# Another order of the last rows of a layered graph kernel, with later steps for the chunk that is third from the end

## What is computed

```python
x = _layernorm(x + relu((adj @ x) @ kernel + bias))
u, v = x, None
for _ in range(3):
    v = mlp_uv(adj @ u)      # three layers 128 -> 128, each with bias and leaky relu
    u = mlp_vu(adj @ v)
return _layernorm(x + v)     # over the 128 features of a node
```

## The kernel before

| row | steps | closes at | hid1 | hid2 | out | statistics |
|---|---|---|---|---|---|---|
| 4 | LAST | 1500 | 1506 | 1510 | 1514 | 1516 |
| 3 | LATE2 | 1516 | 1520 | 1523 | 1525 | 1528 |
| 1 | LATE | 1524 | 1527 | 1529 | 1531 | 1538 |
| 2 a | END | half of the last block | 1535 | 1539 | 1543 | 1549 |

## Time and profile before

### The profile page before, as it was taken

How to read it: one execution, slowest core, us unless ns; L and a number is a source line. 1 busy time by engine, 2 the same in 40 slices (tenths; PEclk the granted TensorE clock), 3 DMA queues, 4 the chain that set the end, 5 groups by cost and what they waited for, 6 DMA issues and landing times.

```text
span 1167.5 us, 13724 instructions
## 1 busy us (share of the span) xinstructions
PE 1153.9 (99%) x5242; PEld 953.5 (82%) x5242; DVE 737.0 (63%) x889; ACT 660.1 (57%) x813; POOL 3.3 (0%) x8
## 2 busy tenths in 40 slices
PE   7999999999999999999999999999999999999997
PEld 6888888888888888888888888888888888887876
DVE  7997676458555555555545746553566555678984
ACT  7765555346554555555444754554556544667874
POOL 0000000000000000000000000000000000000001
PEclk9999999999999999999999999999999999999999
DMA  9988775568366646555656736555564656589871
GB/s 383 403 308 321 246 271 193 204 216 288 120 207 215 213 154 212 204 191 180 211 186 216 246 115 220 205 183 184 196 237 166 212 190 225 173 296 359 309 269 36
DMA packets 72353, 261.60 MB, mean 224 GB/s; under 512 B 8032, under 2 KB 8800, under 8 KB 71264
## 3 DMA queue, kind: packets, MB, share of 16 engines
q1 hardware_dynamic: 72144, 260.61, 63.0%
q10 hardware_dynamic: 144, 0.13, 0.0%
HBM read 258.61 MB, written 2.10 MB: 223 GB/s over the span
## 4 chain that ended last, share of the span: by engine, by line
PE 94%; DMA 3%; DVE 2%; ACT 0%; SPq 0%; issue 0%; ACTq 0%
PE agg_ps L923 28%; PE agg_ps L916 28%; PE agg_ps L909 28%; PE pre_ps L820 4%; DMA adj_raw<-in_adj 3%; PE hid_ps L781 1%; PE hid_ps L783 1%; PE hid_ps L782 1%; DVE adj_lo L761 1%; PE hid_ps L842 1%; PE hid_ps L856 0%; ACT adj_hi L628 0%; DVE stats L641 0%; SPq L490 0%; PE hid_ps L859 0%
## 5 line engine op out<-in xcount | busy, mean ns | idle before, releaser
L761 DVE TENSOR_TENSOR adj_lo<-adj_raw,adj_hi 128x1024 fp32r<-128x1024 f32 x464 | 548.1, 1221 | 224.6 <-ACT adj_hi L628 219.2
L909 PE MATMUL agg_ps<-adj_hi,feat_hi 128*128 128x512 f32 x1484 | 586.4, 395 | 7.3 <-ACT adj_hi L628 7.3
L916 PE MATMUL agg_ps<-adj_hi,feat_lo 128*128 128x512 f32 x1484 | 579.2, 390 | 0.0
L628 ACT ACTIVATE adj_hi<-adj_raw 128x1024 fp32r<-128x1024 f32 x464 | 467.6, 1051 | 82.2 <-PE agg_ps L923 69.1
L923 PE MATMUL agg_ps<-adj_lo,feat_hi 128*128 128x512 f32 x1484 | 459.0, 391 | 0.2 <-DVE adj_lo L761 0.2
L909 PEld LDWEIGHTS agg_ps<-adj_hi,feat_hi 128*128 128x128 f32 x1484 | 279.4, 188 | 65.8 <-issue 9.2
L916 PEld LDWEIGHTS agg_ps<-adj_hi,feat_lo 128*128 128x128 f32 x1484 | 279.5, 188 | 59.3 <-issue 1.9
L923 PEld LDWEIGHTS agg_ps<-adj_lo,feat_hi 128*128 128x128 f32 x1484 | 278.8, 188 | 59.9 <-DVE adj_lo L761 1.5
L522 ACT ACTIVATE hid<-hid_ps,params 128x512 f32<-128x512 f32 (+2 forms) x82 | 55.2, 673 | 61.3 <-PE hid_ps L783 50.7
L593 ACT ACTIVATE in_hi<-part 128x512 fp32r<-128x512 f32 x24 | 15.2, 634 | 110.4 <-DVE part L750 110.4
L522 ACT ACTIVATE post<-pre 128x512 f32<-128x512 f32 x39 | 24.7, 633 | 88.0 <-DVE pre L728 88.0
(11 more groups left out here) (80 smaller groups left out, 389.4 us busy)
## 6 DMA issues: line engine op xcount, KB each, us to landing
adj_raw<-in_adj SPq DMA_DIRECT2D x472, 512.0 KB, 5.6
adj_raw<-in_adj SPq DMA_DIRECT2D x8, 1024.0 KB, 8.1
resid<-in_x SPq DMA_DIRECT2D x8, 256.0 KB, 8.0
out<-resid SPq DMA_DIRECT2D x7, 256.0 KB, 5.2
params<-in_weights SPq DMA_DIRECT2D x1, 386.0 KB, 4.9
b_row<-in_bias_rows SPq DMA_DIRECT2D x1, 128.0 KB, 5.4
out<-resid SPq DMA_DIRECT2D x2, 64.0 KB, 1.7
out<-resid ACTq DMA_DIRECT2D x1, 128.0 KB, 2.0
```

The lines of the kernel that those rows point to most:

```text
L628: act.activation(split_hi(b)[:, i * CHUNK:(i + pieces) * CHUNK], adj_raw[:, h % RAW, 0:pieces * CHUNK], ACT.Copy).then_inc(adj_hi_ready, 1)
L761: dve.tensor_tensor(split_lo(b)[:, slot], adj_raw[:, h % RAW, 0:pieces * CHUNK], split_hi(b)[:, slot].bitcast(F32), ALU.subtract).then_inc ...
L909: pe.matmul(group_bank(g), feat_hi[feats][:, tile(src, i)], split_hi(b)[:, piece(i)], start=start, stop=False)
L916: pe.matmul(group_bank(g), feat_lo[feats][:, tile(src, i)], split_hi(b)[:, piece(i)], start=False, stop=False)
```

## The change

The order of the last rows is 6, 1, 5, 4, 3, 2. So row 1 becomes an ordinary chunk behind row 6, and the last three chunks are rows 4, 3 and 2. `LATE2` has its steps wider apart, `LATE` its statistics and root earlier. The biases of the last three units come behind their second layers. Unit a gets its reciprocal by `dve_root`, is normalised on GpSimd, and ScalarE then issues its DMA at a step `act_out`.

```diff
-    LATE2: dict(dve_sum=0, act_in=1, pe_hid1=4, act_hid1=5, pe_hid2=7, act_hid2=8, pe_out=9, dve_pre=10,
-                act_post=10, dve_stats=12, act_std=14, dve_shift=15, act_norm=16),
+    LATE2: dict(dve_sum=0, act_in=0, pe_hid1=5, act_hid1=6, pe_hid2=9, act_hid2=10, pe_out=13, dve_pre=13,
+                act_post=14, dve_stats=15, act_std=18, dve_shift=18, act_norm=22),
     LATE: dict(dve_sum=0, act_in=1, pe_hid1=1, act_hid1=2, pe_hid2=3, act_hid2=5, pe_out=5, dve_pre=7, act_post=7,
-               dve_front=8, dve_total=8, dve_stats=12, act_std=17, dve_root=18, pool_norm=18),
-    END: dict(dve_sum=0, act_in=0, pe_hid1=1, pe_bias=5, act_hid1=3, pe_hid2=5, act_hid2=7, pe_out=9, act_post=10,
-               dve_stats=15, act_std=19, dve_shift=21, act_norm=24),
-    END2: dict(dve_sum=0, act_in=0, pe_hid1=4, pe_bias=5, act_hid1=6, pe_hid2=8, act_hid2=10, pe_out=12,
+               dve_front=8, dve_total=8, dve_stats=9, act_std=12, dve_root=13, pool_norm=13),
+    END: dict(dve_sum=0, act_in=0, pe_hid1=1, act_hid1=3, pe_hid2=5, act_hid2=7, pe_bias=7, pe_out=8, act_post=10,
+               dve_stats=15, act_std=19, dve_root=20, pool_norm=20, act_out=24),
+    END2: dict(dve_sum=0, act_in=0, pe_hid1=4, act_hid1=6, pe_hid2=8, act_hid2=10, pe_bias=10, pe_out=12,
                act_post=16, dve_stats=18, act_std=21, dve_norm=24),
 }
-LAST_ROWS = (6, 5, 4, 3, 1, 2)
+LAST_ROWS = (6, 1, 5, 4, 3, 2)
...
-            first = TILES if plan.on_pool(u) else 0
+            first = TILES if plan.steps_of(u) == LATE else 0
...
-                    sp.wait_ge(pool_normed, 1)
+                    sp.wait_ge(pool_normed, normed_on_pool(u))
...
-                    if plan.steps_of(u) == END:
-                        act.wait_ge(act_normed, normed_by(u, False))
-                        act.dma_start(out[chunk_of(u)][:, own(u)], resid[:, columns_of(u)]).then_inc(out_written, 16)
+                u = at(t, "act_out", (LAST,))
+                if u is not None:
+                    act.wait_ge(pool_normed, normed_on_pool(u))
+                    act.dma_start(out[chunk_of(u)][:, own(u)], resid[:, columns_of(u)]).then_inc(out_written, 16)
...
                 u = at(t, "dve_root", (LAST,))
                 if u is not None:
+                    tiles = slice(*plan.units[u][2])
                     dve.wait_ge(std_ready, norms(u) + 1)
-                    dve.reciprocal(moments(u)[1], std[:, :]).then_inc(rstd_ready, 1)
+                    wait_for_normed(dve, plan.first_of(u) - 1)
+                    dve.reciprocal(moments(u)[1][:, tiles], std[:, tiles]).then_inc(rstd_ready, 1)
```

More of the change, by code:

```diff
@@ L447, in normed_by, with normed_on_pool @@
                        for i in range(u + 1))
+        def normed_on_pool(u):
+            return sum(plan.on_pool(i) for i in range(u + 1))
         def moments(u):
-            first = TILES if plan.on_pool(u) else 0
+            first = TILES if plan.steps_of(u) == LATE else 0
             return mean_var[:, first:first + TILES, :], rstd[:, first:first + TILES]
```

## The result

| | median us | runs | against before |
|---|---|---|---|
| kernel before | 1169.41 | 22 | |
| changed kernel | 1171.06 (1170.81 to 1171.66) | 22 | 1.0014 (1.0009 to 1.0020) |

The changed kernel is 1.65 us slower, 0.14%: a difference that is clear of the noise, and smaller than the 0.2% that the forecast took as its bound. The profiled execution took 1171.15 us, its span is 1169.3.

What follows compares the result with a forecast made beforehand. TensorE's instructions end to end, its waits and the tail were taken to bound the kernel. Products ending at 1160.27 plus a tail of 8.54 gave a span of 1168.81, +1.31, so 1170.6 us; range 1168.4 to 1171.9.

Steps and rivals of the forecast that it cites:

- Rival D: Row 4's first layer, 0.07 us to spare: one split late makes TensorE wait 1.1 us, time 1171.7; chance 0.10.
- The wait at row 3: Row 4's statistics go ahead of row 3's sum, so TensorE stands 1.59 us before row 3's first layer.
- The wait in the final block: Row 3's statistics go ahead of unit a's sum, making that sum and its first layer 1.12 us later.
- F: Start of the final block, 1154.99 in the kernel before; forecast to move by +0.76 us.
- G: End of TensorE's products, 1158.39 in the kernel before; forecast to move by +1.88 to 1160.27.
- The tail: From the last product to the end of the span: 9.11 us before, forecast 8.54.
- no longer share the way: Tail: row 3's 256 KB leave well before the last three DMAs; 0.2 us off, bounds 0 and 0.35.
- Unit a on GpSimd: Tail: unit a normalised by G + 6.32, its DMA issued at about G + 6.36 instead of G + 6.76.
- Row 3's statistics earlier: Tail: empties VectorE's queue behind G, but GpSimd's four normalisations weren't last; worth 0 by itself.
- C: Row 3 and unit a: sums go once products are through, F moves by -0.28, time 1168.5; chance 0.12.
- E: New wait at row 3: TensorE's clock falls from 2.4 to 1.2 GHz, time about 1181; chance 0.03.
- B: Tail: GpSimd and VectorE exclude each other, unit b's normalisation is held, tail 9.4, time 1171.5; chance 0.16.

Runs made afterwards that it cites:

- third experiment: Changed kernel with row 4's statistics behind row 3's sum, row 3's behind the sums of units a, b, c, unit a normalised on ScalarE; 1169.26 us (0.9999).
- fifth experiment: Changed kernel with unit a alone moved back from GpSimd to ScalarE; 1171.04 us, ratio 1.0014 against the kernel before.
- eighth kernel: The third experiment's kernel with row 3's first layer one tick later, second at 1528, third at 1530; 1168.66 us, repeated 1168.51.
- second experiment: Changed kernel with row 3's statistics at tick 1538, behind the sums of units a, b and c; 1170.66 us, ratio 1.0009 against the kernel before.

## Why the prediction was right, point by point

- **The moved row costs nothing.** The rows in the new order are as fast as in the old one once the steps fit it (third experiment). Rival D, a late row 4, had only 0.07 us to spare, and didn't come (row 4's sum starts at 1134.74, its first layer at 1135.62, 0.88 for the 0.80 that are needed): TensorE's list of waits has two, at row 3 and at unit a. With the order alone, where row 4's first layer is one tick closer still, it does wait, 0.25 us.
- **The wait at row 3** was worked out as 5.21 us from line 826 to line 862, of which TensorE stands for 1.59; the trace has 5.21 and 1.58, and moving the statistics gave 1.0 back of the 1.04 forecast.
- **The wait in the final block** was worked out as a sum at F + 2.74; the trace has F + 2.73.
- **F and G** were to move by 0.76 and 1.88; they moved by 0.88 and 1.98. The missing 0.1 was there before the changed stretch: row 6's first layer is 0.11 us later in this execution than in the one before (1092.99, 1092.88). From there G moved by 1.87.
- **The tail was sized wrongly.** One step that failed is the 0.2 us for DMAs that "no longer share the way": with row 3's DMA issued 2.5 us ahead of the last one (1164.37) the end came 2.40 us behind the last issue, against 2.35 before, and not 2.15. The other is which issue is the last. The forecast went by unit a's on ScalarE, at G + 6.36; it was unit c's on SyncE, at G + 6.53. Unit c was to gain 0.38 and gained 0.23: the third layer of a came at G + 1.57 and not 1.47, and VectorE's normalisations of b and c took 0.38 and 0.43 us beside GpSimd, 0.35 and 0.34 in the fifth experiment without it. Together 0.4 us: 8.93 for 8.54, just under the 9 from which the forecast would have called itself wrong. With the 0.1 of G that is the way from 1170.6 to 1171.06. Nothing cancelled here: both misses went the same way.
- **Unit a on GpSimd** was forecast as 0.4 together with the biases at the issue of its DMA, and brought 0.31; on ScalarE the kernel takes the same time. **The biases** alone gave 0.19 at the third layer, where 0.29 were forecast, and nothing at the end.
- **Row 3's statistics earlier** were put at 0 for the tail, since GpSimd's normalisations weren't last. That left out SyncE, which issues unit b's and c's DMAs only behind row 3's. Third and fifth experiment differ in both statistics and not in unit a: row 3's DMA is issued at G + 5.91 and G + 4.00, c's at G + 6.76 and G + 6.57, and the tails are 9.21 and 8.94 (1169.3 less 1160.36). So the early statistics are worth 0.2 to 0.3 in the tail, and they cost 1.1 ahead of it.
- Of the rivals, C had the sums not held back. The third experiment makes it so (with unit a on ScalarE): counted from row 6's first layer the final block begins 0.22 earlier than before, for 0.28 by C. But it takes 1169.26 and not C's 1168.5, as its tail is 9.21 us and not 8.54. That the eighth kernel is at 1168.5 to 1168.7 is no point for C's sum, since it has row 3's layers moved as well. E, the clock, didn't happen: the windows of 1140 to 1150 and 1150 to 1160, with stands of 1.4 and 1.0 us, have a granted clock of 1.00, as the two rows show.

```profile
1140.00:1150.00 10.00, 8.58 (x40) 6.47 (x39) 3.70 (x14) 2.31 (x4) 0.00 (x0) 1.00 0.00 0
1150.00:1160.00 10.00, 9.05 (x53) 7.60 (x52) 3.54 (x12) 3.31 (x8) 0.00 (x0) 1.00 0.07 26
```

B, the shared ports, would have held unit b's normalisation until GpSimd was done, at 1166.79; it ran from 1165.91 for 0.38 us. The Trainium skill, page "SBUF — State Buffer", section "Who interferes with whom", says that where VectorE needs the shared ports, the engine that issues first has them for the whole instruction and the other blocks. This trace doesn't bear it out for the normalisations, as the earlier trace rows didn't for the add: unit c's began at 1166.44, inside GpSimd's second one, and was through at 1166.87, 0.08 after GpSimd. VectorE was slower by 0.03 and 0.09 us than in the fifth experiment, not held. Whether its normalisation needs the shared ports no row shows.

## What to carry to other kernels

Where every engine issues in a fixed order, a step that nobody waits for (here statistics) must stand behind one that the busiest engine waits for (here a sum), and spreading steps can bring the two into the wrong order as easily as closing them up. Work out for each such wait when the producer's queue reaches it, not only when its data are there: this gave both waits to a few hundredths of a microsecond. An early start for an end step is worth its gain in the tail (0.2 to 0.3 us) less what it delays in front of it (1.1 us). And the engine that issues the last DMAs is such a queue too: follow the end to the DMA that is issued last, and to what stands ahead of it there.

## What the runs showed that I had not expected

- GpSimd's normalisations and VectorE's instructions slow each other by parts, not by whole instructions: four of GpSimd took 3.12 to 3.38 us, VectorE's 128x128 add 0.26 alone and 0.26 to 0.35 beside GpSimd, its normalisation 0.34 or 0.35 alone and 0.38 and 0.43 beside GpSimd. When it is the one and when the other isn't settled.
- From unit a's DMA issue on ScalarE to the end of the span the kernels took 2.35 (before), 2.48 (changed) and 2.58 us (biases alone). From unit c's on SyncE it is 2.35 to 2.47 in all of them but one: in the second experiment, where c's went out 0.7 us ahead of a's, the end came 2.1 behind a's. A gain of 0.1 to 0.2 us at unit a isn't seen at the end unless unit c's DMA is issued earlier as well.
